# A graph attention kernel whose copies of the probabilities and first loads go out on two DMA queues, with sums and scalings moved ahead and another order at the end

## The chip, the cores and the metric

One Trainium2 chip, one of its cores. The metric is the time of one execution in microseconds (us); lower is better. A core has TensorE (PE in the profile), VectorE (DVE), ScalarE (ACT), GpSimd (POOL) and SyncE (SP), which run side by side and wait for each other on semaphores. SyncE computes nothing: it issues DMAs.

## The reference

128 graphs of 64 nodes, 512 features, 16 heads of 32. `adj` says which nodes see each other. Everything is float32, and all four biases are used.

```python
q = heads(x @ Wq + bq); k = heads(x @ Wk + bk); v = heads(x @ Wv + bv)
scores = jnp.einsum('bhqd,bhkd->bhqk', q, k) / sqrt(32)
scores = jnp.where(mask[:, None] == 0, -jnp.inf, scores)
attn = jax.nn.softmax(scores, axis=-1)
out = jnp.einsum('bhqk,bhkd->bhqd', attn, v)          # then the heads side by side
x = _layernorm(x + out @ Wo + bo)                     # no scale, no shift
```

## The kernel before

The 8192 rows are cut into 64 **tiles** of 128 rows (two graphs each). Four tiles make a group, for which q and k are projected together. Float32 products are made of three matmuls on a high and a low part (`split_matmul`, L252 to L254). The program is written out per engine; the order of each engine's instructions is the order of the code, and semaphores tie them together. There is no scheduler.

A tile c goes through these steps:

- PE `project_v`, `project_k`, `project_q` (L252 to L254); ACT `read_k` (L464) and `read_q` (L455) and DVE `read_v` (L546) take the results out of PSUM.
- PE `score` (L303); DVE `mask` (L554 adds the mask, L562 takes the row maximum); POOL `centre` (L706); ACT `exp` (L470); DVE `sum_up` (L566 sum, L569 reciprocal); POOL `normalise` (L163); DVE `turn` (L574, transposes 32x32 blocks).
- SP `place` (L189) issues eight DMAs of 64 KB that put the blocks of probabilities into the big zeroed buffer `pt`; PE `mix` (L317) multiplies it by v, and waits for all eight.
- ACT `read_ot` (L475, high part), DVE `split_ot` (L578, low part), PE `project_out` (L329, L330, L333).
- SP `load_row` (L195) fetches the rows of x, POOL `add_bo` (L701) adds the bias, DVE `add_row` (L585, L588, L591) adds the projection and takes mean and variance, POOL `make_rstd` (L711, L714), DVE `norm_row` (L595), SP `store` (L199).

The loop runs over 30 **slots** p, each with the tiles a = 2p and b = 2p + 1. In slot p PE scores a and b, mixes a-2 and b-2, and projects v for a and b, k and q for a+4 and b+4, and the output for a-2 and b-2. Tiles 60 to 63 have an end written out by hand. SP's queue holds, in this order, loads of adj and x (every second slot), store(a-3), place(a), load_row(b), place(b), store(a-2), load_row(b+1). The first loads (four pieces each of wq and x, then wk, biases, wv, adj, wo, x) are also SP's. `row` has four buffers: load_row(c) waits until tile c-4 is stored.

Of the kernel before, what the change touches and what calls it, by code (L numbers as in the profile page):

```python
# [39 lines left out]
def attention_kernel(nc, xt_dram, x_dram, adj_dram, w_dram, b_dram, out_dram):  # L40
    ctx = ExitStack()
    with ctx:
# [32 lines left out]
        stats = sb("stats", [P, 4, 6])  # L75
        moments = sb("moments", [P, 4, 2])
        shifted = sb("shifted", [P, 4, 1])
        rstd = sb("rstd", [P, 4, 1])
# [12 lines left out]
        row_in = [sem(f"row_in{n}") for n in range(4)]  # L91
        stored = [sem(f"stored{n}") for n in range(4)]
# [8 lines left out]
        turned = sem("turned")  # L101
# [33 lines left out]
        def ot_bank(c):  # L135
            if 2 * FULL <= c < 2 * FULL + 2:
                return psum_s[:, c % 2, 0, :]
            if c >= 2 * FULL + 2:
                return ring[c % 2][:, :]
            return at(c // 2 + 1, c % 2)  # L140
# [13 lines left out]

        def by_row_head(ap):
            return ap.rearrange("p b h k -> p h b k")
# [4 lines left out]
        def normalise(eng, ops, c):  # L161
            eng.wait_ge(inverted, c + 1)
            ops.tensor_tensor(soft_of(c), soft_of(c), on_keys(inverse[:, c % 2, :]), ALU.mult).then_inc(normed, 1)  # L163

        def by_graph(ap):
            return ap.rearrange("p (g k) -> p g k", k=NODES)

# [3 lines left out]
        def _(sp):  # L171
# [10 lines left out]
            def place(c):  # L182

                sp.wait_ge(turned, c + 1)
                wait_for(sp, mixed, c - 1)
                for q in range(P // SQ):
                    for k in range(2):
                        to = q // 2 * NODES + k * SQ
                        sp.dma_start(pt[to:to + SQ, c % 2, q, :, :],  # L189
                                     soft_of(c)[q * SQ:(q + 1) * SQ, k, :, :]).then_inc(pt_in[c % 2], DMA)  # L190

            def load_row(c):
                if c >= 4:
                    sp.wait_ge(stored[c % 4], DMA * (c // 4))
                sp.dma_start(row[:, c % 4], x_dram[c]).then_inc(row_in[c % 4], DMA)  # L195

            def store(c):
                sp.wait_ge(row_done, c + 1)
                sp.dma_start(out_dram[c], row[:, c % 4]).then_inc(stored[c % 4], DMA)  # L199

            for kc in range(KC):
                sp.dma_start(w_raw[0][:, kc, :], w_dram[0][:, kc, :]).then_inc(wq_in[kc], DMA)
                sp.dma_start(x_raw[:, kc, :], xt_dram[0, :, kc, :]).then_inc(x0_in[kc], DMA)
                if kc == 0:
                    for dst, src in zip((bq, bk), b_dram):
                        sp.dma_start(dst[:, :], src).then_inc(qk_b_in, DMA)
            for kc in range(KC):
                sp.dma_start(w_raw[1][:, kc, :], w_dram[1][:, kc, :]).then_inc(wk_in[kc], DMA)
            for dst, src in zip((bv, bo), b_dram[2:]):
                sp.dma_start(dst[:, :], src).then_inc(vo_b_in, DMA)  # L210
# [22 lines left out]
            T = TILES  # L233
            store(T - 7)
            place(T - 4)
            load_row(T - 3)
            place(T - 3)
            place(T - 2)
            place(T - 1)
            store(T - 6)  # L240
            load_row(T - 2)
            store(T - 5)
            load_row(T - 1)
            for c in range(T - 4, T):
                store(c)
# [4 lines left out]
        def _(pe):  # L250
# [179 lines left out]
            pe.wait_ge(row_added, T - 5)  # L430
            mix(T - 2)
            pe.wait_ge(row_added, T - 4)
# [7 lines left out]
        def _(act):  # L440
# [35 lines left out]

            def split_w(n, kc):
# [7 lines left out]

            for kc in range(KC):
# [28 lines left out]
            for p in range(FULL):  # L515
# [6 lines left out]
                for c in (a, b):  # L522
                    if c + 2 * GT < TILES:
                        split_x(c + 2 * GT)
                    read_k(c + GT)
                    read_q(c + GT)
# [3 lines left out]
            for c in range(T - 4, T):  # L530
                exp(c)
            for c in range(T - 4, T):
                read_ot(c)

        @block.vector
        def _(dve):
# [34 lines left out]
            def turn(c):  # L571
                dve.wait_ge(normed, c + 1)
# [9 lines left out]
            def add_row(c):  # L582
                dve.wait_ge(y_proj, c + 1)
                dve.wait_ge(row_biased, c + 1)
                nc.vector.tensor_tensor(row[:, c % 4, :], y_bank(c), row[:, c % 4, :],  # L585
                                        ALU.add).then_inc(row_added, 1)
                dve.wait_ge(row_added, c + 1)
                nc.vector.bn_stats(stats[:, c % 4, :], row[:, c % 4, :]).then_inc(row_stats, 1)  # L588
                dve.wait_ge(row_stats, c + 1)
                dve.sem_inc(dve_went_on, 1)  # L590
                nc.vector.bn_aggr(moments[:, c % 4, :], stats[:, c % 4, :]).then_inc(row_moments, 1)  # L591

            def norm_row(c):
                dve.wait_ge(row_rstd, c + 1)
                nc.vector.tensor_scalar(row[:, c % 4, :], row[:, c % 4, :], moments[:, c % 4, 0:1],  # L595
                                        rstd[:, c % 4, :], ALU.subtract, ALU.mult).then_inc(row_done, 1)
# [23 lines left out]
            for p in range(FULL):  # L620
# [20 lines left out]
                if p >= 1:  # L641
                    norm_row(a - 2)
# [7 lines left out]
            norm_row(T - 7)  # L650
            sum_up(T - 4)
            sum_up(T - 3)
# [9 lines left out]
            add_row(T - 5)  # L662
            turn(T - 1)
            norm_row(T - 6)
            norm_row(T - 5)
            read_v(T - 2)
            read_v(T - 1)
            split_ot(T - 4)
            split_ot(T - 3)
            add_row(T - 4)  # L670
            add_row(T - 3)
            split_ot(T - 2)
            norm_row(T - 4)
            split_ot(T - 1)
            norm_row(T - 3)
            add_row(T - 2)
            norm_row(T - 2)
            add_row(T - 1)
            norm_row(T - 1)

        @block.gpsimd
        def _(pool):
# [16 lines left out]
            def add_bo(c):  # L699
                pool.wait_ge(row_in[c % 4], DMA * (c // 4 + 1))  # L700
                nc.gpsimd.tensor_tensor(row[:, c % 4, :], row[:, c % 4, :], bo[:, :],  # L701
                                        ALU.add).then_inc(row_biased, 1)
# [6 lines left out]
            def make_rstd(c):  # L709
                pool.wait_ge(row_moments, c + 1)  # L710
                nc.gpsimd.tensor_tensor(shifted[:, c % 4, :], moments[:, c % 4, 1:2], eps[:, :],  # L711
                                        ALU.add).then_inc(row_shifted, 1)
                pool.wait_ge(row_shifted, c + 1)
                nc.gpsimd.tensor_tensor(rstd[:, c % 4, :], shifted[:, c % 4, :], minus_half[:, :],  # L714
# [18 lines left out]
            for p in range(FULL):  # L733
# [21 lines left out]
            add_bo(T - 4)  # L755
# [3 lines left out]
            centre(T - 1)  # L759
            add_bo(T - 3)  # L760
            normalise(pool, nc.gpsimd, T - 2)
            normalise(pool, nc.gpsimd, T - 1)
            make_rstd(T - 6)
            make_rstd(T - 5)
            add_bo(T - 2)
            add_bo(T - 1)
            for c in range(T - 4, T):
                make_rstd(c)

# [33 lines left out]
```

## Time and profile before

| | us |
|---|---|
| median of 3 runs | 880.45 |
| lowest, highest | 876.42, 881.17 |
| the profiled execution, time | 879.76 |
| its span, first to last instruction | 878.0 |

The profile is one execution. Its span leaves 1.8 us of its time outside. Busy times are of one engine; an engine that waits is not busy, and PE's matmuls overlap, so that a stretch in which PE shows no gap is one in which it is never waited for. The timeline's rows give the start and the length of a piece of work, and in brackets how long the engine had been idle before it and what ended that. A row of the SP queue (SPq) is the issuing of a DMA, not its transfer.

### The profile page before, as it was taken

How to read it: one execution, taken by the hardware profiler on the slowest of the kernel's cores; microseconds unless marked ns; L12 is line 12 of the kernel's file. 1: busy time of each engine (PE TensorE's matmuls, PEld its weight loads, DVE VectorE, ACT ScalarE, POOL GpSimd, SP SyncE). 2: the span in 40 equal slices, each digit the busy share in tenths (PEclk: the TensorE clock that was granted, in tenths of full speed). 3: DMA queues.
4: the chain of work that ended last, by engine and by line, in shares of the span. 5: the costliest groups of instructions: out<-in, count | busy, mean ns of one | idle time of the engine just before them, and what ended most of it. 6: DMA issues, size and time to landing. Idle time of an engine off the chain costs nothing.

```text
span 878.0 us, 17537 instructions
## 1 busy us (share of the span) xinstructions
PE 844.6 (96%) x7177; PEld 690.7 (79%) x7177; DVE 541.0 (62%) x729; ACT 285.5 (33%) x401; POOL 470.9 (54%) x409
## 2 busy tenths in 40 slices
PE   7979899999999999999999999999999999999973
PEld 6857788888888888888888888888888878888852
DVE  4655566655676655576655567665567665557863
ACT  6532333223333323333323333332333332323210
POOL 2254565546666455656545565654565654454632
PEclk9989999999999999999999999999999999999987
DMA  8224224343242433424243342434323243332143
GB/s 311 73 72 125 72 67 136 84 125 110 76 124 78 145 85 90 135 75 125 83 139 97 84 131 64 135 94 138 98 73 123 77 139 86 102 85 66 57 99 105
DMA packets 50143, 91.86 MB, mean 105 GB/s; under 512 B 11280, under 2 KB 13328, under 8 KB 47888
## 3 DMA queue, kind: packets, MB, share of 16 engines
q1 hardware_dynamic: 50064, 90.75, 35.1%
q8 instruction: 57, 0.93, 0.4%
q14 instruction: 22, 0.18, 0.1%
HBM read 40.37 MB, written 16.78 MB: 65 GB/s over the span
## 4 chain that ended last, share of the span: by engine, by line
PE 89%; DVE 3%; SPq 2%; DMA 2%; issue 2%; POOL 1%; ACT 1%; POOLq 0%; DVEq 0%; ACTq 0%
PE ring L252 20%; PE ring L253 19%; PE ring L254 19%; PE ring L317 6%; PE psum_s L303 6%; PE ring L329 6%; PE ring L333 6%; PE ring L330 6%; SPq L189 2%; DMA qt<-in_wq 1%; DMA row<-in_x 1%; DMA out_rows<-row 1%; DVE soft L554 1%; DVE top L562 0%; ACT kt L464 0%
## 5 line engine op out<-in xcount | busy, mean ns | idle before, releaser
L585 DVE TENSOR_TENSOR row<-ring,row 128x512 f32<-128x512 f32 x60 | 40.4, 673 | 207.5 <-PE ring L333 207.5
L701 POOL TENSOR_TENSOR row<-row,bo 128x512 f32<-128x512 f32 x64 | 88.4, 1381 | 138.9 <-DMA row<-in_x 138.9
L706 POOL TENSOR_TENSOR soft<-soft,top 128x1024 f32<-128x1024 f32 x62 | 118.9, 1917 | 80.5 <-DVE top L562 80.5
L163 POOL TENSOR_TENSOR soft<-soft,inverse 128x1024 f32<-128x1024 f32 x62 | 117.6, 1918 | 15.6 <-DVE inverse L569 15.6
L464 ACT ACTIVATE kt<-ring,bk_slot,in_slot 128x512 f32<-128x512 f32 x128 | 92.4, 773 | 81.9 <-PE ring L254 81.9
L252 PE MATMUL ring<-wv_hi,x_hi 128*128 128x512 f32 x256 | 104.0, 406 | 0.0
L252 PE MATMUL ring<-x_hi,wq_hi 128*128 128x512 f32 x256 | 99.8, 390 | 3.3 <-DVE x_lo L607 3.3
L574 DVE STREAM_TRANSPOSE soft<-soft 128x1024 f32<-128x1024 f32 x62 | 77.2, 1245 | 38.7 <-POOL soft L163 38.7
L253 PE MATMUL ring<-wv_lo,x_hi 128*128 128x512 f32 x256 | 101.0, 395 | 0.0
L254 PE MATMUL ring<-wv_hi,x_lo 128*128 128x512 f32 x256 | 100.9, 394 | 0.0
L252 PE MATMUL ring<-x_hi,wk_hi 128*128 128x512 f32 x256 | 99.8, 390 | 0.8 <-ACT kt L464 0.8
L253 PE MATMUL ring<-x_lo,wq_hi 128*128 128x512 f32 x256 | 99.6, 389 | 0.0
L253 PE MATMUL ring<-x_lo,wk_hi 128*128 128x512 f32 x256 | 99.6, 389 | 0.0
L254 PE MATMUL ring<-x_hi,wk_lo 128*128 128x512 f32 x256 | 99.6, 389 | 0.0
L254 PE MATMUL ring<-x_hi,wq_lo 128*128 128x512 f32 x256 | 99.5, 389 | 0.0
L470 ACT ACTIVATE soft<-soft 128x1024 f32<-128x1024 f32 x62 | 65.8, 1062 | 94.7 <-POOL soft L706 94.7
L329 PE MATMUL ring<-wo_hi,ot_hi 128*128 128x512 f32 x240 | 95.6, 398 | 0.0
L475 ACT CAST ot_hi<-ring 128x512 fp32r<-128x512 f32 x62 | 36.4, 587 | 178.6 <-PE ring L317 178.6
L330 PE MATMUL ring<-wo_lo,ot_hi 128*128 128x512 f32 x240 | 94.4, 393 | 0.0
L711 POOL TENSOR_TENSOR shifted<-moments,eps 128x1 f32<-128x1 f32 x64 | 12.2, 190 | 149.9 <-DVE moments L591 149.9
L554 DVE TENSOR_TENSOR soft<-psum_s,bias 128x1024 f32<-128x1024 f32 x62 | 75.6, 1220 | 7.6 <-DMA pt<-soft 7.2
L448 ACT CAST x_hi<-x_raw 128x512 fp32r<-128x512 f32 x60 | 36.6, 614 | 133.9 <-PE ring L254 131.1
(71 smaller groups left out, 1482.0 us busy)
## 6 DMA issues: line engine op xcount, KB each, us to landing
pt<-soft SPq DMA_DIRECT2D x496, 64.0 KB, 2.0
row<-in_x SPq DMA_DIRECT2D x64, 256.0 KB, 2.9
out_rows<-row SPq DMA_DIRECT2D x64, 256.0 KB, 2.3
x_raw<-in_xt SPq DMA_DIRECT2D x15, 1024.0 KB, 7.0
adj<-in_adj SPq DMA_DIRECT2D x16, 128.0 KB, 3.3
qt<-in_wq SPq DMA_DIRECT2D x4, 256.0 KB, 4.3
x_raw<-in_xt SPq DMA_DIRECT2D x4, 256.0 KB, 4.8
kt<-in_wk SPq DMA_DIRECT2D x4, 256.0 KB, 7.0
```

The lines of the kernel that those rows point to most:

```text
L163: ops.tensor_tensor(soft_of(c), soft_of(c), on_keys(inverse[:, c % 2, :]), ALU.mult).then_inc(normed, 1)
L252: nc.tensor.matmul(out, left_hi, right_hi, start=kc == 0, stop=False)
L253: nc.tensor.matmul(out, left_hi, right_lo, start=False, stop=False)
L254: return nc.tensor.matmul(out, left_lo, right_hi, start=False, stop=kc == KC - 1)
L329: nc.tensor.matmul(y_bank(c), ot_hi[:, c % 2, kc, :], w_hi[3][:, kc, :], start=kc == 0, stop=False)
L330: nc.tensor.matmul(y_bank(c), ot_hi[:, c % 2, kc, :], w_lo[3][:, kc, :], start=False, stop=False)
L464: last = nc.scalar.activation(kt[:, buf, m, :, s, :], by_graph(k_bank(J)), ACT.Identity, bias=bk_slot[:, s, m:m + 1], scale=in_slot[:, s:s ...
L470: nc.scalar.activation(soft_of(c), soft_of(c), ACT.Exp, scale=SCALE).then_inc(exped, 1)
L554: nc.vector.tensor_tensor(soft_of(c), psum_s[:, c % 2].rearrange("p r (h b k) -> p (r h) b k", b=2, k=SQ) .rearrange("p h b k -> p b h k") ...
L574: nc.vector.transpose(flat, flat).then_inc(turned, 1)
L701: nc.gpsimd.tensor_tensor(row[:, c % 4, :], row[:, c % 4, :], bo[:, :], ALU.add).then_inc(row_biased, 1)
L706: nc.gpsimd.tensor_tensor(soft_of(c), soft_of(c), on_keys(top[:, c % 2, :]), ALU.subtract).then_inc(centred, 1)
```

## The change

- The eight DMAs of `place` are shared: SP issues the four for q = 0 and 1, ACT the four for q = 2 and 3 (new function `place` on ACT, between the two halves of its slot's projection reads). `mix` waits for all eight as before.
- The first eight loads alternate between SP and ACT. The loads of bq and bk come after wk.
- In a slot, DVE's sum_up(a) comes before read_v(a), norm_row(a-3) after sum_up(b), and POOL's add_bo(a) after the two normalise.
- The end: the four last rows have buffers in `qt` (free once tile 59 is scored) and are loaded at once; stats and moments have eight buffers; DVE scales the probabilities of tile 63; turns come earlier and the additions of rows later; the norms of tiles 58 to 61 are POOL's; mix(62) and mix(63) write to other banks and no longer wait for `row_added`.

```diff
+        def row_of(c):
+            if c >= TILES - 4:
+                return qt[:, 0, c - (TILES - 4), :]
+            return row[:, c % 4, :]
...
+        def norm_row(eng, ops, c):
+            eng.wait_ge(row_rstd, c + 1)
+            ops.tensor_scalar(row_of(c), row_of(c), moments[:, c % 8, 0:1], rstd[:, c % 8, :],
+                              ALU.subtract, ALU.mult).then_inc(row_done, 1)
 # SP
-                for q in range(P // SQ):
+                for q in range(2):
...
             for kc in range(KC):
-                sp.dma_start(w_raw[0][:, kc, :], w_dram[0][:, kc, :]).then_inc(wq_in[kc], DMA)
-                sp.dma_start(x_raw[:, kc, :], xt_dram[0, :, kc, :]).then_inc(x0_in[kc], DMA)
-                if kc == 0:
-                    for dst, src in zip((bq, bk), b_dram):
-                        sp.dma_start(dst[:, :], src).then_inc(qk_b_in, DMA)
+                if kc % 2 == 0:
+                    sp.dma_start(w_raw[0][:, kc, :], w_dram[0][:, kc, :]).then_inc(wq_in[kc], DMA)
+                else:
+                    sp.dma_start(x_raw[:, kc, :], xt_dram[0, :, kc, :]).then_inc(x0_in[kc], DMA)
 ...
             def load_row(c):
+                if c >= TILES - 4:
+                    sp.wait_ge(scored, TILES - 4)
+                    sp.dma_start(row_of(c), x_dram[c]).then_inc(last_row_in[c % 4], DMA)
+                    return
...
             T = TILES
+            load_row(T - 3)
+            load_row(T - 2)
+            load_row(T - 1)
             store(T - 7)
-            place(T - 4)
-            load_row(T - 3)
-            place(T - 3)
-            place(T - 2)
-            place(T - 1)
-            store(T - 6)
-            load_row(T - 2)
-            store(T - 5)
-            load_row(T - 1)
             for c in range(T - 4, T):
+                place(c)
+            for c in range(T - 6, T):
                 store(c)
# PE, the end
-            pe.wait_ge(row_added, T - 5)
             mix(T - 2)
-            pe.wait_ge(row_added, T - 4)
             mix(T - 1)
# ACT
+            def place(c):
+                act.wait_ge(turned, c + 1)
+                wait_for(act, mixed, c - 1)
+                for q in range(2, 4):
+                    for k in range(2):
+                        to, of = block_of(c, q, k)
+                        act.dma_start(to, of).then_inc(pt_in[c % 2], DMA)
 ...
+            for kc in range(KC):
+                if kc % 2 == 0:
+                    act.dma_start(x_raw[:, kc, :], xt_dram[0, :, kc, :]).then_inc(x0_in[kc], DMA)
+                else:
+                    act.dma_start(w_raw[0][:, kc, :], w_dram[0][:, kc, :]).then_inc(wq_in[kc], DMA)
# DVE, a slot
+                sum_up(a)
+                if p >= 1:
                     read_v(a)
+                sum_up(b)
                 if p >= 2:
-                    norm_row(a - 3)
-                sum_up(a)
-                sum_up(b)
+                    norm_row(dve, nc.vector, a - 3)
# DVE, the end
             mask(T - 2)
+            turn(T - 4)
             mask(T - 1)
-            turn(T - 4)
+            turn(T - 3)
             read_v(T - 3)
-            turn(T - 3)
             sum_up(T - 2)
             sum_up(T - 1)
-            add_row(T - 6)
+            normalise(dve, nc.vector, T - 1)
             turn(T - 2)
# POOL, a slot
-                add_bo(a)
                 normalise(pool, nc.gpsimd, a)
                 normalise(pool, nc.gpsimd, b)
+                add_bo(a)
 # POOL, the end
-            for c in range(T - 4, T):
+            for c in range(T - 6, T - 2):
                 make_rstd(c)
+                norm_row(pool, nc.gpsimd, c)
+            make_rstd(T - 2)
+            make_rstd(T - 1)
```

The order of the instructions at the three places that matter most. First ACT in slot 0, before: `x_hi` is split_x(8) and (9), `kt` read_k, `qt` read_q of tiles 4 and 5.

```order
L448 CAST x_hi<-x_raw 128x4x128 [waits q_proj,v_proj,x_in]
L464 ACTIVATE kt<-ring,bk_slot,in_slot 128x8x64 [waits k_proj]
L464 ACTIVATE kt<-ring,bk_slot,in_slot 128x8x64
L455 ACTIVATE qt<-ring,bq 128x512 [waits q_proj]
L448 CAST x_hi<-x_raw 128x4x128 [waits q_proj,v_proj]
L464 ACTIVATE kt<-ring,bk_slot,in_slot 128x8x64 [waits k_proj]
L464 ACTIVATE kt<-ring,bk_slot,in_slot 128x8x64
L455 ACTIVATE qt<-ring,bq 128x512 [waits q_proj]
```

No DMA stands between them.

ACT in slot 0 with the change: the four rows of DMA for tile 0 and for tile 1 stand ahead of the second half.

```order
L465 CAST x_hi<-x_raw 128x4x128 [waits q_proj,v_proj,x_in]
L481 ACTIVATE kt<-ring,bk_slot,in_slot 128x8x64 [waits k_proj]
L481 ACTIVATE kt<-ring,bk_slot,in_slot 128x8x64
L472 ACTIVATE qt<-ring,bq 128x512 [waits q_proj]
L501 DMA pt<-soft 32x512 [waits turned]
L501 DMA pt<-soft 32x512 x3
L501 DMA pt<-soft 32x512 [waits turned]
L501 DMA pt<-soft 32x512 x3
L465 CAST x_hi<-x_raw 128x4x128 [waits q_proj,v_proj]
L481 ACTIVATE kt<-ring,bk_slot,in_slot 128x8x64 [waits k_proj]
L481 ACTIVATE kt<-ring,bk_slot,in_slot 128x8x64
L472 ACTIVATE qt<-ring,bq 128x512 [waits q_proj]
```

Split_x(9), read_k(5) and read_q(5) now come behind two waits for `turned`.

ACT at the end, before: read_ot(58) and (59), exp of tiles 60 and 61 (`soft`), of 62 and 63 (`x_raw`), then the four read_ot.

```order
L475 CAST ot_hi<-ring 128x512 [waits y_proj,mixed] x2
L470 ACTIVATE soft<-soft 128x1024 [waits centred] x2
L470 ACTIVATE x_raw<-x_raw 128x1024 [waits centred] x2
L475 CAST ot_hi<-psum_s 128x512 [waits y_proj,mixed] x2
L475 CAST ot_hi<-ring 128x512 [waits y_proj,mixed] x2
```

The first row is read_ot(58) and (59); all DMAs of the place are SP's here.

ACT at the end with the change, from the exp of tiles 60 and 61.

```order
L487 ACTIVATE soft<-soft 128x1024 [waits centred] x2
L501 DMA pt<-soft 32x512 [waits mixed,turned]
L501 DMA pt<-soft 32x512 x3
L487 ACTIVATE x_raw<-x_raw 128x1024 [waits centred]
L501 DMA pt<-soft 32x512 [waits mixed,turned]
L501 DMA pt<-soft 32x512 x3
L487 ACTIVATE x_raw<-x_raw 128x1024 [waits centred]
L492 CAST ot_hi<-psum_s 128x512 [waits y_proj,mixed]
L501 DMA pt<-x_raw 32x512 [waits mixed,turned]
L501 DMA pt<-x_raw 32x512 x3
L492 CAST ot_hi<-psum_s 128x512 [waits y_proj,mixed]
L501 DMA pt<-x_raw 32x512 [waits mixed,turned]
```

Each `place` stands between an exp or a read_ot and the next; exp(62) is now behind the wait for tile 60's turn.

DVE near the end, before: the norms of tiles 58 and 59 (first row), read_v(62) and (63), the low parts and the rows of tiles 60 and 61.

```order
L595 TENSOR_SCALAR row<-row,moments,rstd 128x512 [waits row_rstd] x2
L546 TENSOR_TENSOR v<-ring,bv 128x512 [waits mixed,v_proj] x2
L578 TENSOR_TENSOR ot_lo<-psum_s,ot_hi 128x512 [waits ot_hi_done] x2
L585 TENSOR_TENSOR row<-psum_s,row 128x512 [waits row_biased,y_proj]
L588 BN_STATS stats<-row 128x6 [waits row_added]
L591 BN_AGGR moments<-stats 128x2 [waits row_stats]
L585 TENSOR_TENSOR row<-psum_s,row 128x512 [waits row_biased,y_proj]
L588 BN_STATS stats<-row 128x6 [waits row_added]
L591 BN_AGGR moments<-stats 128x2 [waits row_stats]
L578 TENSOR_TENSOR ot_lo<-ring,ot_hi 128x512 [waits ot_hi_done]
L595 TENSOR_SCALAR row<-row,moments,rstd 128x512 [waits row_rstd]
L578 TENSOR_TENSOR ot_lo<-ring,ot_hi 128x512 [waits ot_hi_done]
```

The last two rows are the norm of tile 60 and the low part of tile 63.

DVE there with the change: it starts with the scaling of tile 63.

```order
L176 TENSOR_TENSOR x_raw<-x_raw,inverse 128x1024 [waits inverted]
L621 STREAM_TRANSPOSE x_raw<-x_raw 128x1024 [waits normed]
L625 TENSOR_TENSOR ot_lo<-psum_s,ot_hi 128x512 [waits ot_hi_done]
L621 STREAM_TRANSPOSE x_raw<-x_raw 128x1024 [waits last_normed]
L625 TENSOR_TENSOR ot_lo<-psum_s,ot_hi 128x512 [waits ot_hi_done]
L590 TENSOR_TENSOR v<-ring,bv 128x512 [waits mixed,v_proj] x2
L632 TENSOR_TENSOR row<-ring,row 128x512 [waits row_biased,y_proj]
L634 BN_STATS stats<-row 128x6 [waits row_added]
L637 BN_AGGR moments<-stats 128x2 [waits row_stats]
L632 TENSOR_TENSOR row<-ring,row 128x512 [waits row_biased,y_proj]
L634 BN_STATS stats<-row 128x6 [waits row_added]
L637 BN_AGGR moments<-stats 128x2 [waits row_stats]
```

No row of norms is left here; the turns of tiles 62 and 63 stand ahead of read_v and of all rows, and the rows of 58 and 59 behind them.

## Rows read from the trace of the kernel before

**Rows 1.** Stretches; length, busy time of each engine, granted clock, DMA share, GB/s

```profile
9.00:10.00 1.00, 0.88 (x4) 0.78 (x5) 1.00 (x2) 0.59 (x1) 0.00 (x0) 1.00 0.89 229
...
56.00:58.00 2.00, 0.00 (x0) 0.00 (x0) 0.00 (x0) 0.00 (x0) 2.00 (x2) 0.50 0.43 98
...
400.00:600.00 200.00, 200.00 (x1754) 164.83 (x1747) 130.47 (x176) 66.65 (x93) 116.64 (x98) 1.00 0.35 103
```

**Rows 2.** Timeline of the SP queue, start; start us, us, engine line op

```profile
4.95 0.43 SPq L203 DMA_DIRECT2D x_raw<-in_xt  x1
...
46.25 5.03 SPq L189 DMA_DIRECT2D pt<-soft  x8
```

**Rows 3.** Timeline of ACT, start; in brackets the idle time before

```profile
10.94 0.62 ACT L484 CAST wq_hi<-qt 128x512 fp32r<-128x512 f32 x1 [1.35 <-DMA qt<-in_wq]
```

**Rows 4.** Timeline of PE, start to tile 2

```profile
13.05 0.47 PE L252 MATMUL ring<-x_hi,wq_hi 128*128 128x512 f32 x1 [0.94 <-DVE x_lo L607]
...
14.28 0.39 PE L254 MATMUL ring<-x_hi,wq_lo 128*128 128x512 f32 x1
...
58.39 1.93 PE L317 MATMUL ring<-pt,v 128*32 128x128 f32 x32 [4.54 <-issue]
60.25 0.80 PE L252 MATMUL ring<-wv_hi,x_hi 128*128 128x512 f32 x1
...
62.51 0.40 PE L254 MATMUL ring<-wv_hi,x_lo 128*128 128x512 f32 x1
```

**Rows 5.** Timeline of PE, 86 to 92 us

```profile
89.99 0.65 PE L317 MATMUL ring<-pt,v 128*32 128x128 f32 x5 [2.72 <-issue]
```

**Rows 6.** Timelines of DVE, SP, ACT and PE, one slot in the middle

```profile
413.77 1.25 DVE L574 STREAM_TRANSPOSE soft<-soft 128x1024 f32<-128x1024 f32 x1 [0.63 <-POOL soft L163]
418.84 4.94 SPq L189 DMA_DIRECT2D pt<-soft  x8
420.05 1.45 ACT L464 ACTIVATE kt<-ring,bk_slot,in_slot 128x512 f32<-128x512 f32 x2 [2.10 <-PE ring L254]
427.36 1.96 PE L317 MATMUL ring<-pt,v 128*32 128x128 f32 x64
```

**Rows 7.** Timeline of PE, the end

```profile
839.84 1.08 PE L317 MATMUL psum_s<-pt,v 128*32 128x128 f32 x32 [1.38 <-issue]
845.56 1.93 PE L317 MATMUL psum_s<-pt,v 128*32 128x128 f32 x32 [4.64 <-issue]
...
868.77 2.08 PE L333 MATMUL psum_s<-wo_hi,ot_lo 128*128 128x512 f32 x4 [4.31 <-DVE ot_lo L578]
```

**Rows 8.** Timeline of the SP queue, the end

```profile
845.85 11.13 SPq L189 DMA_DIRECT2D pt<-x_raw  x16
```

**Rows 9.** Timeline of POOL, the end

```profile
842.64 3.78 POOL L163 TENSOR_TENSOR x_raw<-x_raw,inverse 128x1024 f32<-128x1024 f32 x2
...
865.50 1.26 POOL L701 TENSOR_TENSOR row<-row,bo 128x512 f32<-128x512 f32 x1 [2.00 <-DMA row<-in_x]
```

**Rows 10.** The page, part 5: the exponential, all of it

```profile
L470 ACT ACTIVATE soft<-soft 128x1024 f32<-128x1024 f32 x62 | 65.8, 1062 | 94.7 <-POOL soft L706 94.7
```

**Rows 11.** One line of the kernel, the mask of a group: durations

```profile
L696 POOL TENSOR_SCALAR bias<-adj x16: 1077/1084/1093, 18.8 to 778.1; 128x256 f32<-128x256 int32 x16
```

**Rows 12.** Timeline of DVE, the end

```profile
836.41 1.16 DVE L566 TENSOR_REDUCE total<-x_raw 128x16 f32<-128x1024 f32 x1
...
844.58 1.25 DVE L574 STREAM_TRANSPOSE x_raw<-x_raw 128x1024 f32<-128x1024 f32 x1 [5.12 <-POOL x_raw L163]
...
867.57 0.55 DVE L595 TENSOR_SCALAR row<-row,moments,rstd 128x512 f32<-128x512 f32 x1 [9.86 <-POOL rstd L714]
...
869.09 0.69 DVE L585 TENSOR_TENSOR row<-psum_s,row 128x512 f32<-128x512 f32 x1
...
870.65 0.18 DVE L591 BATCH_NORM_AGGREGATE moments<-stats 128x2 f32<-128x6 f32 x1
...
874.89 0.55 DVE L595 TENSOR_SCALAR row<-row,moments,rstd 128x512 f32<-128x512 f32 x1 [0.93 <-POOL rstd L714]
```

More of the change, by code:

```diff
@@ L74, in attention_kernel @@
         inverse = sb("inverse", [P, 2, HEADS])
[L75 to L78, printed above, removed]
+        stats = sb("stats", [P, 8, 6])
+        moments = sb("moments", [P, 8, 2])
+        shifted = sb("shifted", [P, 8, 1])
+        rstd = sb("rstd", [P, 8, 1])
         eps = sb("eps", [P, 1])
@@ L91, in attention_kernel @@
         row_in = [sem(f"row_in{n}") for n in range(4)]
+        last_row_in = [sem(f"last_row_in{n}") for n in range(4)]
         stored = [sem(f"stored{n}") for n in range(4)]
@@ L521, in _ @@
                 exp(b)
[L522 to L526, printed above, removed]
+                if a + 2 * GT < TILES:
+                    split_x(a + 2 * GT)
+                read_k(a + GT)
+                read_q(a + GT)
+                place(a)
+                place(b)
+                if b + 2 * GT < TILES:
+                    split_x(b + 2 * GT)
+                read_k(b + GT)
+                read_q(b + GT)
             T = TILES
@@ L529, in _ @@
             read_ot(T - 5)
-            for c in range(T - 4, T):
-                exp(c)
-            for c in range(T - 4, T):
-                read_ot(c)
+            exp(T - 4)
+            exp(T - 3)
+            place(T - 4)
+            exp(T - 2)
+            place(T - 3)
+            exp(T - 1)
+            read_ot(T - 4)
+            place(T - 2)
+            read_ot(T - 3)
+            place(T - 1)
+            read_ot(T - 2)
+            read_ot(T - 1)
         @block.vector
@@ L584, in add_row @@
                 dve.wait_ge(row_biased, c + 1)
-                nc.vector.tensor_tensor(row[:, c % 4, :], y_bank(c), row[:, c % 4, :],
-                                        ALU.add).then_inc(row_added, 1)
+                nc.vector.tensor_tensor(row_of(c), y_bank(c), row_of(c), ALU.add).then_inc(row_added, 1)
                 dve.wait_ge(row_added, c + 1)
-                nc.vector.bn_stats(stats[:, c % 4, :], row[:, c % 4, :]).then_inc(row_stats, 1)
+                nc.vector.bn_stats(stats[:, c % 8, :], row_of(c)).then_inc(row_stats, 1)
                 dve.wait_ge(row_stats, c + 1)
                 dve.sem_inc(dve_went_on, 1)
[L591 to L596, printed above, removed]
+                nc.vector.bn_aggr(moments[:, c % 8, :], stats[:, c % 8, :]).then_inc(row_moments, 1)
             def split_w(n, kc):
@@ L641, in _ @@
                 if p >= 1:
-                    norm_row(a - 2)
+                    norm_row(dve, nc.vector, a - 2)
             T = TILES
@@ L699, in add_bo @@
             def add_bo(c):
[L700 to L702 removed]
+                if c >= TILES - 4:
+                    pool.wait_ge(last_row_in[c % 4], DMA)
+                else:
+                    pool.wait_ge(row_in[c % 4], DMA * (c // 4 + 1))
+                nc.gpsimd.tensor_tensor(row_of(c), row_of(c), bo[:, :], ALU.add).then_inc(row_biased, 1)
             def centre(c):
@@ L754, in _ @@
             centre(T - 3)
-            add_bo(T - 4)
             normalise(pool, nc.gpsimd, T - 4)
@@ L759, in _ @@
             centre(T - 1)
+            add_bo(T - 4)
+            normalise(pool, nc.gpsimd, T - 2)
             add_bo(T - 3)
[L761 to L764, printed above, removed]
             add_bo(T - 2)
             add_bo(T - 1)
-            for c in range(T - 4, T):
+            for c in range(T - 6, T - 2):
                 make_rstd(c)
+                norm_row(pool, nc.gpsimd, c)
+            make_rstd(T - 2)
+            make_rstd(T - 1)
 def kernel(x, adj, L0_gnn_Wq, L0_gnn_bq, L0_gnn_Wk, L0_gnn_bk, L0_gnn_Wv, L0_gnn_bv, L0_gnn_Wo, L0_gnn_bo):
```

51 lines of the change are left out of this document (28 added, 23 removed).

## The prediction

> **What bounds the kernel now.** I read the busy time by stretches first. In the middle PE is the bound: from 400 to 600 us it is busy for 200.00 of 200 us at full clock [rows 1], and DVE, ACT and POOL have room. The reader should see that no saving on them can shorten that stretch. PE waits for more than 1.5 us in three places only, found in its timeline. At the start the four pieces of wq and x come in one by one; the last piece of wq lets ACT go on at 10.94 us, and PE's first matmul on it starts at 13.05 [rows 3, 4]. In slot 1 mix(1) starts after 4.54 us of idle PE, in slot 2 some matmuls of a mix after 2.72 [rows 4, 5]. And in the end mix(61) comes after 4.64 us, and the last part of project_out(62) after 4.31 [rows 7].
>
> The waits of slot 1 and of the end have one cause. A tile's eight copies go out one after another on SP, 0.6 us each: those of tile 0 take 5.03 us from 46.25, then a row load and the eight of tile 1 follow, and 2.1 us after the start of the last one (56.3) mix(1) starts at 58.39 [rows 2, 4]. The last 16 copies of the kernel take 11.13 us of SP's time [rows 8]. The last wait is another: the loads of rows 62 and 63 queue on SP behind stores, POOL adds the bias at 865.50, and DVE sits 9.86 us before norm_row(60), with the low part of tile 62 behind it, which PE waits for [rows 7, 9, 12].
>
> **The change, part by part.** The sum is made against the profiled execution, 879.76 us for a span of 878.0; the median of the runs, 880.45, is 0.7 above it. Times below are on the clock of the trace before. I take the four issues of each queue at the 0.63 us of SP, side by side: 2.5 us a tile.
>
> *First loads.* The last of the eight is issued at 4.95 [rows 2]; with four on each queue that would be about 2.4 us sooner, the upper end. But from 9 to 10 us the DMA engines are busy for 0.89 of the time and move 229 GB/s [rows 1]: the pieces wait for transfers, not for issues. Lower end 0. I take 1.0, nearer to the busy engines. The table load of ACT now follows its four issues and is done when the first piece arrives; bq and bk come later, with about 5 us to spare before PE asks for q(0) out of PSUM. Nothing for either. The Trainium skill (DMA: Bandwidth & Descriptors, section on issuing engines) speaks against a gain here: all queues run on the same 16 DMA engines, and a second one saves issue time only. By that rule this term is 0.
>
> *Slot 0 and 1.* Normalise(0) no longer waits for add_bo(0), so turn(0) and the first copies move from 46.25 to 45.8. SP then issues four copies, the row, four copies: to 51.4, the last begun at 50.8 and landed 2.1 later, at 52.9. ACT issues its eight from 45.8 to 50.8, and only then splits x(9) (0.62) and reads k(5) (1.45, as in rows 6): 52.9. Mix(1) needs both, and PE reaches it at 53.4, after the scores and mix(0). So it starts 5.0 us sooner. There is more: in the idle time the granted clock fell to 0.50, that is from 2.4 to 1.2 GHz, after PE had been idle for some 3 us [rows 1], mix(1) took 1.93 for what takes 1.08 at the end of the trace [rows 4, 7], and the five matmuls from 60.25 took 2.26 us where those from 13.05 took 1.23 [rows 4]. Without the gap that is 1.9 us. **Slot 1: 6.9 us**, 5.0 if the clock still falls.
>
> *Slot 2.* The 2.72 us have the releaser "issue", in the midst of a mix, while x of a later group is loading: no data was missing. PE's own instructions do not change there. The loads of x now go out some 4 us sooner against PE, so the pause may stay or go. With the slow matmuls behind it, it is worth 0 to 3.9; I take the middle, 1.9, since no row is near either end.
>
> *The middle slots.* Nothing gained: PE has no wait. Is the cover kept? In the slot shown turn(b) ends at 415.0 and ACT's next work that waits for PE, read_k(b+4), starts at 420.05 after 2.10 us of idle [rows 6]. With sums and scalings moved ahead turn(a) ends about 412.6, so ACT's eight issues (5.0) run to 417.7 or so, split_x(b+8) follows, and ACT is free 1.7 us before read_k is due. SP has fewer issues than before. POOL's add_bo(a) moves behind 3.8 us of scaling [rows 9], and its sum is asked for in the next slot. Cost 0.
>
> *The end.* PE works without a wait until 838.5 (839.84 less 1.38) [rows 7]. Then:
>
> 1. Turn(60) moves ahead of mask(63), to 831.0; both queues issue to 833.6; landed by 835.7. Mix(60) starts at 838.5.
> 2. Turn(61) ends at 834.5, its copies have landed at 839.2. Mix(61) starts at 839.5, not at 845.56.
> 3. ACT does exp(63) behind these copies, to 838.3 (1.06) [rows 10]; DVE adds up (1.4 with the reciprocal) and scales tile 63 itself (1.2, as its turn of the same size) instead of waiting for two scalings of POOL, 3.78 [rows 9, 12]; the turns of 62 and 63 end at 842.3 and 844.2, not at 845.8 and 848.6.
> 4. ACT: copies of 62, read_ot(61) to 845.4, copies of 63 to 847.9; landed at 849.9, where the last landed at about 858.5 before.
> 5. PE: project_out(60) to 844.0, (61) to 848.2, mix(62), mix(63) to 850.9, project_out(62) to 853.8, (63) to 856.8.
> 6. DVE, from 846.1: two read_v 1.3, five add_row of 1.7 (869.09 to 870.83) [rows 12], two split_ot 0.7 each. The moments of tile 58 are there at 849.1, those of 62 at 857.3.
> 7. POOL then does rstd (0.9 with its wait, the idle time before the last norm) and norm_row for four tiles in a row. The trace has no such norm on POOL. The nearest rows are its addition of the same width, 1.26, and its tensor_scalar of half that width, 1.08 [rows 9, 11]; twice the latter, 2.2, is the upper end, 1.08 the lower. I take 1.3, the same width. Norm(61) ends at 857.7, rstd(62) at 858.5; DVE then has norm 0.5, add_row(63) 1.7 and a wait of 0.9, and the last norm starts at 861.7, not at 874.89.
>
> The store behind the last norm is as before. **The end: 13.2 us**; 9.6 with a norm of 2.2, 13.6 with 1.08 (DVE is then the bound).
>
> **Sum:** 1.0 + 6.9 + 1.9 + 13.2 = 23.0, so 879.8 - 23.0 = 856.8, **857 us**. With all lower ends (0, 5.0, 0, 9.6) it is 865.2, with all upper ends (2.4, 6.9, 3.9, 13.6) 853.0.
>
> **The rivals.**
>
> - *Nothing at the start.* The loads are bound by transfers alone: 857.8. For it the 0.89 [rows 1]; against it, 229 GB/s is little for engines so busy, and two queues may mix better. Chance 0.20. By the Trainium skill's page on DMA, section on issuing engines, it would be this one.
> - *Dear norms on POOL.* At 2.2 us each they hold the end: 860.4. Chance 0.12.
> - *More pauses like that of slot 2.* PE now runs from tile 0 without the idle time of slot 1, in which its instructions could catch up. Three more at 3.9 give about 869. Against it: one such pause over 1 us in 30 slots. Chance 0.06.
> - *Issuing is shared.* If the two queues slow each other, and an issue costs twice 0.63, ACT is done with the copies of tile 1 at 55.9 and with k(5) at 57.9 (gain 0.5), the last copies are issued at 857.6, and the last norm starts about 867.8 (gain 7.1): 872. No row shows two queues at once. Chance 0.14.
> - *The copies do not land sooner.* If landing, not issuing, sets the pace of 0.6 us a copy, the change does not do what it says: 877 to 880. Against it, 64 KB each 0.63 us is 104 GB/s, and the same engines moved 229. Chance 0.04.
> - *Slower: ACT's queue blocks the middle.* Behind the two waits for `turned` and the eight issues stand split_x(b+8) and read_k(b+4), and the next slot's second mix, at 428.3 (halfway through the pair at 427.36) [rows 6], waits for that k. The issues start at 412.6, 2.1 us of work follow, so they may take 13.6 us: 1.7 each. Beyond that each slot stalls. At 2.0 us each it is 2.4 us in each of 29 slots, +70, less what the end keeps: about 920. For it: no row shows ACT issuing. Against it: SP's issues stay near 0.6, 4.94 for eight [rows 6]. Chance 0.04.
>
> **How the numbers follow.** The forecast has 0.40, the others as given; the sum is 1. A measurement of this kernel tells 0.5%, 4.4 us, from no change. Faster by more than that: 0.92; within: 0.04; slower: 0.04. The range goes from 852, one below the upper ends, to 870, which takes in the dear norms, the pauses and the near part of the shared issuing.
>
> **What would show it.** Mix(1) within 1 us of mix(0), no clock of 0.50 before 800 us unless at slot 2, ACT's DMA issues 0.5 to 0.7 us, read_k(b+4) in the middle still waiting for PE, PE's gaps behind 838 adding up to under 4 us in place of 13, and a chain at the end that runs through POOL's norms. Wrong if ACT's issues last over 1 us, if PE shows gaps in the middle slots, or if the piece of wq that comes last still comes at 10.9 and slot 1 still waits.

## The result, and the profile after

The changed kernel takes **859.12 us** (median of four executions, 857.66 to 859.69) where the kernel before takes 880.21 (four, 876.42 to 881.17): a ratio of 0.9769, 95% interval 0.9740 to 0.9799. It is faster by 21 us, and 2.1 us above the 857.0 that was predicted. Measured again later it took 859.66 (six executions) beside 875.74 of the kernel before (eleven, 874.14 to 882.07): 0.9794, interval 0.9757 to 0.9830. The kernel before has executions near 875 (six of these eleven) and others near 880, its profiled one, 879.76, among them, so that the gain is 16 us by the later measurement and 21 by the first.

The profiled execution of the change took 857.66 us with a span of 855.9, 22.1 less than the 878.0 before. I split both spans where PE starts the scores of a pair of tiles, which it does once in each slot:

| stretch (us) | before | after | gain | predicted |
|---|---|---|---|---|
| start to the first score | 33.64 | 32.38 | 1.26 | 1.0 |
| slot 0 | 16.85 | 16.83 | 0.02 | 0 |
| slot 1 | 32.94 | 25.96 | 6.98 | 6.9 |
| slot 2 | 30.51 | 25.96 | 4.55 | 1.9 |
| the other slots (25.96 each, but one of 26.88 and 26.30) | | | 0.58 | 0 |
| the end, from the last full pair's score (815.78, 802.39) | 62.19 | 53.47 | 8.7 | 13.2 |

So the sum came out by luck, by two errors that cancel: slot 2 gave 2.65 more than its term, the end 4.5 less.

**Start.** The windows of the changed kernel, one in the first loads and one in the middle (columns as in [rows 1]):

```profile
9.00:10.00 1.00, 1.00 (x6) 0.81 (x5) 0.62 (x2) 0.31 (x1) 0.00 (x0) 1.00 1.06 402
...
386.60:586.60 200.00, 200.00 (x1760) 165.08 (x1760) 130.02 (x175) 66.03 (x92) 116.59 (x98) 1.00 0.34 101
```

Between 9 and 10 us the DMA engines now move 402 GB/s, not 229. In the middle nothing moved: PE is busy for all of the 200 us. ACT's timeline at the start answers to [rows 3]:

```profile
2.12 0.64 ACTq L516 DMA_DIRECT2D qt<-in_wq  x1
2.79 1.28 ACT L510 ACT_TABLE_LOAD   x1 [2.79 <-issue]
4.74 0.62 ACT L510 CAST wq_hi<-qt 128x512 fp32r<-128x512 f32 x1 [0.67 <-DMA qt<-in_wq]
...
9.69 0.62 ACT L510 CAST wq_hi<-qt 128x512 fp32r<-128x512 f32 x1 [0.88 <-DMA qt<-in_wq]
...
14.51 1.26 ACT L472 ACTIVATE qt<-ring,bq 128x512 f32<-128x512 f32 x2 [1.47 <-POOL bk_slot L769]
```

The first piece is split later than before (4.74 for 3.87), the last one 1.25 us sooner. The last row shows a new wait: bk is issued later, and ACT waits 1.47 us for what POOL makes of it. PE does not.

**Slot 0 to 1.** Both queues and PE, which answer to [rows 2, 4]:

```profile
44.31 2.49 SPq L207 DMA_DIRECT2D pt<-soft  x4
...
47.47 2.51 SPq L207 DMA_DIRECT2D pt<-soft  x4
```

```profile
44.31 5.39 ACTq L501 DMA_DIRECT2D pt<-soft  x8
49.80 0.62 ACT L465 CAST x_hi<-x_raw 128x512 fp32r<-128x512 f32 x1 [5.73 <-PE ring L273]
50.33 1.44 ACT L481 ACTIVATE kt<-ring,bk_slot,in_slot 128x512 f32<-128x512 f32 x2
```

```profile
49.80 1.38 PE L322 MATMUL psum_s<-kt,qt 64*64 64x128 f32 x44
51.11 1.95 PE L336 MATMUL ring<-pt,v 128*32 128x128 f32 x64
```

Two queues issue side by side at 0.63 and 0.67 us each, and mix(0) and mix(1) run as one group of 64 matmuls, with no idle time and at full clock.

**The end.** The chain of waits of the changed kernel from 821 us (start, us, what), a part of it:

```profile
821.09 0.52 ACTq L501
821.63 0.87 ACTq L501
822.53 0.62 ACTq L501
823.18 0.62 ACTq L501
823.84 1.07 ACT x_raw L487
824.94 1.23 DVE total L610
826.19 0.26 DVE inverse L613
826.48 2.13 DVE x_raw L176
828.61 1.17 DVE x_raw L621
...
832.62 0.59 ACT ot_hi L492
...
837.79 2.08 POOL row L183
...
840.78 2.08 POOL row L183
...
843.76 2.08 POOL qt L183
...
846.73 2.08 POOL qt L183
```

exp(63) stands behind four copies on ACT, DVE's scaling of tile 63 takes 2.13 us (1.92 on POOL), and four norm_rows of 2.08 us follow each other on POOL. On DVE the last norm comes out of that chain, after 5.07 us of idle time:

```profile
849.64 0.55 DVE L183 TENSOR_SCALAR qt<-qt,moments,rstd 128x512 f32<-128x512 f32 x1 [5.07 <-POOL rstd L755]
...
852.77 0.55 DVE L183 TENSOR_SCALAR qt<-qt,moments,rstd 128x512 f32<-128x512 f32 x1 [0.93 <-POOL rstd L755]
```

PE in the end, answering to [rows 7]:

```profile
825.00 1.95 PE L336 MATMUL psum_s<-pt,v 128*32 128x128 f32 x64
...
830.39 1.19 PE L352 MATMUL psum_s<-wo_hi,ot_lo 128*128 128x512 f32 x4 [1.38 <-DVE ot_lo L625]
...
833.26 0.50 PE L348 MATMUL psum_s<-wo_hi,ot_hi 128*128 128x512 f32 x1 [1.67 <-ACT ot_hi L492]
...
838.34 1.08 PE L336 MATMUL ring<-pt,v 128*32 128x128 f32 x32 [1.01 <-DMA pt<-x_raw]
```

The waits for mixes 60 and 61 are gone. Three are left, 4.06 us in all, two of them new: split_ot(60) stands behind turn(62) on DVE, and read_ot(61) behind the copies of tile 62 on ACT.

### The profile page after: what moved, and what is told of

It is laid out like the page before. It is cut to its first block, busy times and chain, and to the rows that moved or that the text cites. A ratio compares the mean times of both kernels' runs of the same rounds, so it can differ in the third digit from the quotient of the medians.

```text
span 855.9 us, 17597 instructions
## 1 busy us (share of the span) xinstructions
PE 837.0 (98%) x7177; PEld 686.9 (80%) x7177; DVE 540.7 (63%) x726; ACT 284.5 (33%) x401; POOL 480.3 (56%) x412
## 4 chain that ended last, share of the span: by engine, by line
PE 91%; DVE 4%; POOL 2%; issue 1%; DMA 1%; ACTq 1%; ACT 1%; POOLq 0%; DVEq 0%
PE ring L271 20%; PE ring L272 19%; PE ring L273 19%; PE psum_s L322 6%; PE ring L336 6%; PE ring L348 6%; PE ring L352 6%; PE ring L349 6%; DMA qt<-in_wq 1%; ACTq L501 1%; DVE soft L598 1%; POOL qt L183 0%; POOL row L183 0%; DVE top L606 0%; DVE total L610 0%
## 5 line engine op out<-in xcount | busy, mean ns | idle before, releaser
L176 POOL TENSOR_TENSOR soft<-soft,inverse 128x1024 f32<-128x1024 f32 x62 | 123.3, 1989 | 25.1 <-DVE inverse L613 22.1
L743 POOL TENSOR_TENSOR row<-row,bo 128x512 f32<-128x512 f32 x60 | 78.8, 1313 | 38.5 <-DMA row<-in_x 38.5
```

What stands on the lines that cost most here:

```text
L743: nc.gpsimd.tensor_tensor(row_of(c), row_of(c), bo[:, :], ALU.add).then_inc(row_biased, 1)
```

## The experiments

**x1: first loads on two queues, alone** (in the kernel before).

```diff
+                if kc % 2 == 0:
+                    act.dma_start(x_raw[:, kc, :], xt_dram[0, :, kc, :]).then_inc(x0_in[kc], DMA)
+                else:
+                    act.dma_start(w_raw[0][:, kc, :], w_dram[0][:, kc, :]).then_inc(wq_in[kc], DMA)
```

(SP keeps the other four, and bq and bk move behind wk, as in the change.)

> The kernel before with the first eight loads on two queues and bq, bk after wk, nothing else. Theory (issuing sooner brings the pieces sooner): the first score starts at 32.4 us in place of 33.64, as in the changed kernel, and the rest is as before: slot 1 still 32.9 us from score to score, the end still 62 us behind the last slot's score; span about 876.7. Rival (transfers alone bind, and the 1.3 us in the changed kernel came from something else): first score at 33.6, span 878. The pause of slot 2 (4.55 us) should be there in both, if it comes with the idle time of slot 1; if it depends on chance it may be gone.

One execution: 880.66 us, span 878.9, no sooner than the kernel before. The first score is at 33.22 (33.64 before), not at the 32.4 that I had put, and ACT's timeline has the gain at its last piece:

```profile
9.76 0.62 ACT L485 CAST wq_hi<-qt 128x512 fp32r<-128x512 f32 x1 [0.70 <-DMA qt<-in_wq]
```

What it gained is lost in slot 2, where the pause is still there and the clock stays low behind it:

```profile
89.57 0.65 PE L318 MATMUL ring<-pt,v 128*32 128x128 f32 x5 [2.98 <-issue]
90.15 0.80 PE L253 MATMUL ring<-wv_hi,x_hi 128*128 128x512 f32 x1
```

One trace is too little for 1 us. Over all profiles of this study the last piece of wq is split at 10.52 to 11.05 us in the four kernels with one queue, at 9.36 to 9.76 in the six with two, and the first score is at 33.29 to 33.79 (mean 33.57) and at 32.08 to 33.22 (mean 32.67). The ranges do not overlap, though those of the first score are only 0.07 us apart: the difference of the means, 0.9 us, is what the term is worth here.

**x2: copies on two queues, alone** (in the kernel before; ACT's order as in the change, first loads, DVE, POOL and row buffers as before).

```diff
-                for q in range(P // SQ):
+                for q in range(2):
...
+            def place(c):
...
+                for q in range(2, 4):
```

> The kernel before with the eight copies of a tile shared by SP and ACT and ACT's order as in the changed kernel; loads, DVE, POOL and PE as before. Theory (serial issuing on one queue made the wait of slot 1): slot 1 takes 26.0 us from score to score in place of 32.94, mix(1) right behind mix(0), no clock of 0.50 there; in the end the last block is issued 5.6 us sooner, and with it the loads of rows 62 and 63, so the end is about 5 us shorter. Together 12 us, and 16.5 if the pause of slot 2 goes too: 864 to 868. Rival (the sums and scalings moved ahead made the gain): slot 1 keeps a gap of over 3 us, time over 873.

862.64 us (862.31 to 865.32; four executions, beside 877.24 of the kernel before in seven), ratio 0.9830, interval 0.9790 to 0.9869. The span is 860.1, so the copies alone bring 17.9 of the 22.1 us between the profiled executions: slot 1 lasts 26.78, slot 2 26.83, the end 54.76 (7.4 less than before). That is below my 864 to 868, mostly because the end gives 7.4 and not 5. Of the 17.9 us 3.7 are the pause of slot 2, which is not the same in every execution (see x6). PE's timeline has what is left in slots 1 and 2:

```profile
54.01 1.08 PE L317 MATMUL ring<-pt,v 128*32 128x128 f32 x32 [0.61 <-DMA pt<-soft]
...
81.48 0.42 PE L317 MATMUL ring<-pt,v 128*32 128x128 f32 x5 [0.46 <-issue]
```

**x3: the change with all copies on SP.**

```diff
-                for q in range(2):
+                for q in range(4):
...
-                place(a)
-                place(b)
```

(ACT's place goes altogether.)

> The changed kernel with all eight copies of a tile on SP, ACT issuing none of them; everything else as changed. Theory: slot 1 is long again (32.3 to 32.9 us from score to score, mix(1) some 4 us behind mix(0), clock 0.50), 6.5 us lost there; the middle stays at 25.96 us a slot; the end loses 3 us on mix(61) and mix(63), but its last norm hangs on the four norms on POOL, so it loses 0 to 3 us. If the pause of slot 2 comes with the idle time of slot 1, 4.5 more. Time 866 to 873. Rival (the sharing does nothing, the earlier sums do all): 859.

865.50 us (864.37 to 870.63; four executions), ratio 0.9864, interval 0.9822 to 0.9907; span 862.6. Slot 1 is at 31.92 again. The time is just under my 866 to 873, since the end got shorter. The idle time before mix(1) is back, and with it the low clock:

```profile
56.13 1.94 PE L336 MATMUL ring<-pt,v 128*32 128x128 f32 x32 [4.19 <-issue]
...
836.98 1.24 PE L336 MATMUL psum_s<-pt,v 128*32 128x128 f32 x32 [2.98 <-issue]
```

The surprise is the end. PE waits 2.98 us before mix(61), and yet the end lasts 52.26 us, 1.2 less than with two queues. exp(63) starts 19.51 us after the last full pair's score, against 21.45 in the change, since no copies stand ahead of it on ACT, and DVE's scaling of tile 63 takes 1.55 us, not 2.13: the turns of 62 and 63 end 2.5 us sooner. The second queue helps PE in the end, but PE does not set the end.

**x5: the idle time of slot 1 filled** (the kernel before with 18 matmuls whose results nobody reads, ahead of mix(1); one execution, 874.50 us, span 872.7). Does the low clock cost 1.9 us there?

```diff
+                if p == 1:
+                    for _ in range(18):
+                        nc.tensor.matmul(ring[1][:, :], w_hi[3][:, 0, 0:P], w_hi[3][:, 0, :], start=True, stop=True)
                 mix(b - 2)
```

> The kernel before with 18 matmuls of 128x512 (results unused) on PE between mix(0) and mix(1) in slot 1, about 4.1 us of work inside the wait. Theory of the clock: mix(1) still starts at about 58.4, as its copies come no sooner, but runs at full clock: its 32 matmul records take 1.08 us in place of 1.93, and five matmuls behind it 1.2 in place of 2.26; slot 1 is 1.9 us shorter, 31.0. For the pause of slot 2: if it comes from PE having been idle in slot 1, it is gone and slot 2 takes 25.96 us (span about 871.6); if it comes from the load of x that falls on it, it stays (span about 876).

Slot 1 lasts 32.04, not 31.0. PE's timeline:

```profile
53.93 4.38 PE L387 MATMUL ring<-wo_hi 128*128 128x512 f32 x18
59.47 1.08 PE L317 MATMUL ring<-pt,v 128*32 128x128 f32 x32 [1.16 <-DMA pt<-soft]
60.48 0.50 PE L252 MATMUL ring<-wv_hi,x_hi 128*128 128x512 f32 x1
```

Mix(1) takes 1.08 us where it took 1.93, and five matmuls from 60.48 take 1.26 where [rows 4] have 2.26: together the 1.9 us of the prediction. The size of the clock's cost is shown. But the copies of tile 1 landed 1.1 us later in this execution (SP's eight took 5.83 us, not 4.94), so mix(1) began later and half of it was lost. A second thing was not expected: slot 2 lasts 25.96. Its pause is gone.

**x6: the pause of slot 2.** In the traces of before, x1, x2 and x3 the pause sits at the same matmul of PE, 3.84 us behind the first score of the slot; in x5 it is missing. The queue that brings instructions, q8 (57 packets, 0.93 MB in all, 16 KB each), goes with it: in the four with a pause a packet starts 2.5 to 3.8 us after the first packet of the 1 MB load of x (87.51 against 85.01 in the kernel before), and PE goes on 1.2 to 1.6 us behind the packet's end; in x5 it came at 73.88, long before the load (85.36), in the changed kernel at 73.48, as the load began (73.43). The DMA views of the kernel before, from 80 to 87.3 and from 87.3 to 89 us (issues; packets, MB and share by queue). In the first there is a load of x and no row of q8:

```profile
x_raw<-in_xt SPq DMA_DIRECT2D x1, 1024.0 KB, 7.1
```

In the second there is one packet of it:

```profile
q1 hardware_dynamic: 51, 0.32, 51.7%
q8 instruction: 1, 0.02, 3.3%
```

To test it the load of x for group 3 brings 16 columns; x of tiles 12 to 15 is left out otherwise.

```diff
+                if G == 3:
+                    sp.dma_start(x_raw[:, 0, 0:16], xt_dram[G, :, 0, 0:16]).then_inc(x_in, DMA)
+                    return
```

> The kernel before, in which the 1 MB load of x for group 3 (issued in slot 2) brings 16 of its columns only; it leaves out x of tiles 12 to 15 otherwise. Theory (PE waits for its next block of instructions, which comes behind that load on the same DMA engines): the pause of 2.98 us at 88.9 goes or falls under 0.6, slot 2 lasts 26 to 27.5 us in place of 30.5, slot 1 stays at 32.9. Rival (the pause follows from the idle time and the low clock of slot 1, whatever is loading): slot 2 stays at 30 to 31. The time falls by 3 to 4.5 us by the first, by nothing by the second.

Slot 2 lasts 26.25 us while slot 1 is at 33.51: all but 0.3 us of the pause is gone though the idle time ahead of it is not, and the rival falls. The packet came at 85.10, 1.5 us into the slot, where it came 4.1 us into it in the kernel before. PE's timeline has both mixes of slot 2 as one group, which takes 2.24 us in place of 1.95:

```profile
83.63 1.98 PE L306 MATMUL psum_s<-kt,qt 64*64 64x128 f32 x64
85.54 2.24 PE L320 MATMUL ring<-pt,v 128*32 128x128 f32 x64
```

That a late packet makes the pause is borne out by the other traces: it is short where the packet comes 1.4 to 2.0 us into the slot (x2, x4, x6, x7, a2: slot 2 at 26.24 to 26.83), and long where it comes 2.3 to 4.5 us into it (x3, before, x1: 27.62 to 32.2). That the load makes the packet late is not shown. In x4, x7 and a2 the load stands ahead of the packet, and the packet comes within 0.1 us of where it does in x6. In slot 26 of the kernel before (26.88 us) PE pauses 0.52 us at the same place, and the packet there starts 1.1 us ahead of the load. And a2 is the changed kernel itself, of which the first trace has no pause in slot 2:

```profile
80.12 0.42 PE L336 MATMUL ring<-pt,v 128*32 128x128 f32 x5 [0.28 <-issue]
```

So when the packet comes differs between executions of one kernel, and a single one of x6 can't tell the missing load from that. Its time, 875.22 us, is 4.5 below the profiled execution of before, but equal to those of its eleven that lie near 875. The pause may well be what parts the two sorts of executions; only one execution of the kernel before has a profile, so this is argued and not shown.

**x4: the end's norms on DVE.** The change, but norm_row of tiles 58 to 61 goes from POOL to DVE, each two or three steps behind its add_row; POOL keeps make_rstd.

```diff
-            for c in range(T - 6, T - 2):
+            for c in range(T - 6, T):
                 make_rstd(c)
-                norm_row(pool, nc.gpsimd, c)
-            make_rstd(T - 2)
-            make_rstd(T - 1)
```

> After the change, with all norm_rows of the end on DVE (0.5 us each there) between its additions, and POOL left with make_rstd alone. Theory (the four norms of 2.08 us on POOL, one behind the other, hold the end): the last norm_row starts 3.3 to 3.9 us sooner than 852.77, so the span is about 852.3 and the time about 855.7. Rival (DVE with its additions of 1.7 us is the bound, so what leaves POOL only comes back on DVE): 857.5 or more, no change. PE's part of the end stays as it is, its last matmul at about 845.2.

855.20 us, with 854.72, 855.20 and 855.88 in three executions (a fourth took 1694.79 and is left out), ratio 0.9743, interval 0.9696 to 0.9790; span 852.9. The end lasts 49.82 us, 3.65 less than the change's 53.47, as the theory had it; the rival falls. DVE's timeline:

```profile
842.33 0.53 DVE L183 TENSOR_SCALAR row<-row,moments,rstd 128x512 f32<-128x512 f32 x1
...
849.83 0.55 DVE L183 TENSOR_SCALAR qt<-qt,moments,rstd 128x512 f32<-128x512 f32 x1 [0.71 <-POOL rstd L759]
```

The same operation takes 0.53 us there and 2.08 on POOL. PE's part stays as it was: its last matmul ends 43.1 us after the last full pair's score, in the change 42.8.

**x7: another order of the end, on top of x4.** It is aimed at exp(63), PE's waits and the scaling. The edit against the change, in part:

```diff
-            place(T - 3)
             exp(T - 1)
+            place(T - 3)
             read_ot(T - 4)
-            place(T - 2)
             read_ot(T - 3)
+            place(T - 2)
...
             sum_up(T - 2)
+            turn(T - 2)
             sum_up(T - 1)
-            normalise(dve, nc.vector, T - 1)
-            turn(T - 2)
             split_ot(T - 4)
-            turn(T - 1)
             split_ot(T - 3)
             read_v(T - 2)
             read_v(T - 1)
+            turn(T - 1)
```

(And the scaling of tile 63 back on POOL, all norms on DVE as in x4, in a slightly other order among the additions.)

> After the change, with another order in the end: exp(63) before the copies of tile 61 and read_ot(61) before those of tile 62 on ACT, the scaling of tile 63 on POOL again and DVE's turn(62) before sum_up(63), and all norms on DVE as in the run before. Theory (the end is 3.5 us too long by POOL's norms, and PE waits 1.38, 1.67 and 1.01 us because split_ot(60) stands behind turn(62) and read_ot(61) behind four issues): PE's waits behind mix(61) fall from 4.1 us to 2 or less, the span is about 849 and the time about 852. Rival (PE's waits only move to mix(62) and mix(63), since the turns of 62 and 63 come later): 855 to 856, as with the norms alone.

**853.42 us** (852.22 to 855.36, six executions), ratio 0.9725, interval 0.9691 to 0.9759. It is faster than both kernels: the change beside it took 858.91 to 861.15, and the two sets do not meet (0.993 of its median). The end lasts 46.72 us, another 3.1 less. The waits of PE behind mix(61) fall from 4.06 us to one of 2.40, somewhat more than I had put:

```profile
834.02 1.08 PE L336 MATMUL ring<-pt,v 128*32 128x128 f32 x32
837.51 1.08 PE L336 MATMUL ring<-pt,v 128*32 128x128 f32 x32 [2.40 <-DMA pt<-x_raw]
```

It is mix(63) that waits, 2.40 us where it waited 1.01 in the change: so the rival was right in part. Turn(63) now stands behind both read_v and ends at 832.48, and the copies of tile 63 follow it:

```profile
831.25 1.23 DVE L621 STREAM_TRANSPOSE x_raw<-x_raw 128x1024 f32<-128x1024 f32 x1
```

```profile
828.41 7.56 ACTq L501 DMA_DIRECT2D pt<-x_raw  x8
```

The ACT row spans its eight issues for tiles 62 and 63, with 1.5 us of waiting for that turn between them. The four for tile 63 take 3.45 us, where eight take 5.39 in slot 0.

**a2: the change once more**, for that comparison.

> The changed kernel once more, beside these on the same chip: 857.7 to 859.7 us.

859.66 us (858.91 to 861.15), span 857.9: first score 33.16, slot 2 26.65, end 53.45. The end is the same to 0.02 us in two profiles; the 2 us between the spans are at the start, in slot 2 and in one later slot.

## Why the prediction was right, and where it was not

*First loads, 1.0: right.* 1.26 in the profile, 0.9 over all of them. The rival "nothing at the start" falls. The Trainium skill (DMA: Bandwidth & Descriptors, section "Issuing engines are not separate DMA queues") says that a second engine saves only the time to issue, usually a small one. The traces do not contradict that: the last of the eight issues starts at 2.12 in place of 4.95, and the last piece of wq is split 0.8 to 1.7 us sooner. What they do not bear out is the 0 that the prediction made of it. Whether issues set the gain or the order in which the pieces share the engines was not tried.

*Slot 1, 6.9: right, and for the reason given.* 6.98. x3 has the wait of 4.19 us back with one queue, and x5 shows the clock's part. What x2 leaves of it, 0.61 us before mix(1), is gone in the change, where the sums and scalings come sooner. One reading was off: the granted clock was 0.81 from 55 to 56 us and 0.50 from 56 on, so that it fell some 1.8 us after PE's last work (53.85), not some 3; in x3 it held to about 56.1, 4 us after. ACT was free of its eight copies at 49.7 and of k(5) at 51.8. The rival "issuing is shared" falls, since an issue costs 0.67 us on ACT beside SP, not 1.3, and so does "the copies do not land sooner".

*Slot 2, 1.9: undersized.* 4.55 in the profile against a term of 0 to 3.9. The step that failed is "PE's own instructions do not change there", with the middle taken for want of a row. The instructions do not change, but when a packet of them arrives does, and it sets the pause (the traces under x6). The upper bound was too low as well: without the pause slot 2 is at 25.96, and 30.51 less that was there to be read. Part of the gain is luck: a2, the same kernel, has slot 2 at 26.65, a gain of 3.9. Why the packet comes early in one execution and late in another, and what the load has to do with it, is open. By the Trainium skill (Runtime: NRT & Kernel Launch, section "Instruction fetch mechanics") instructions come in 16 KiB blocks fetched ahead, a cost "mostly hidden"; the middle slots, at 25.96, agree, and the 2.72 and 2.98 us of before and x1 do not. "More pauses" did not come: no later slot is longer than 26.30 us.

*Middle, 0: right.* The slots are at 25.96. ACT's eight issues run from 399.55 to 405.4 in one of them, and read_k then waits 1.14 us for PE: the cover held, with half of the margin it had. The rival of the other sign falls by the 0.73 us of an issue there, against the 1.7 from which it decides. (Its price, "about 920", does not follow from its terms: 879.8 and 70, less all of the 23.0, are 927.)

*The end, 13.2: oversized by 4.5.* Two terms were mis-sized. Norm_row on POOL was taken at 1.3 us, "the same width" as the addition; it is 2.08, near the upper end of 2.2. Four in a row are 3.1 us of the 4.5. x4 takes them away and gains 3.65. The rival "dear norms" is what happened, at its place and price; it was given 0.12 on 860.4. DVE's scaling of tile 63 was taken at 1.2 us "as its turn of the same size"; it is 2.13, more than POOL's 1.92, and the turns come 0.9 and 0.7 later. With them the copies of tile 62 on ACT and read_ot(61) behind them come later (done at 833.2, where my schedule less the 13.4 us by which the two scores differ has 832.0), then split_ot(61), and the moments of tile 58 1.1 us later than worked out. 1.1 and 3.4 (the norms with what lies between them) are the 4.5. The 3.1 us that the end loses once more in x7 came from several moves at once; which of them gave how much was not tried.

*The sum:* 23.0 worked out, 22.1 measured; the errors are +0.3 (start), +0.1, +2.6, +0.6 and -4.5.

*The parts overlap.* Between single profiled executions the copies alone (x2) give 17.9 us, the rest without them (x3) 15.4, and together 22.1; 3.7, 2.9 and 4.6 of these are the pause of slot 2. In the end each gives 7.4 and 9.9, together 8.7: once the copies are quick other things bound the end, and ACT's exp(63) comes 1.9 us later for the copies ahead of it.

## What to carry to other kernels

Before an operation moves to another engine, look for a row of just that operation on that engine: width alone is no guide (the norm: 0.53 us on DVE, 2.08 on POOL; the scaling: 1.92 on POOL, 1.55 to 2.14 on DVE). Where an engine takes over DMA issues, ask what stands behind them in its queue at the end of the program, where nothing else covers them. A pause with no missing data is to be looked for in the instruction queue. And one trace of each kernel is too little for a gain of a few us where such a pause comes and goes.

## What was not expected of the hardware

- A tensor_scalar with two per-partition operands, 128x512, takes 2.08 us on POOL, an addition of two full tensors of that size 1.3.
- A multiplication by a broadcast operand, 128x1024, takes 2.13 us on DVE in the change (2.14 in x4 and a2) and 1.55 in x3, which is unexplained; on POOL it takes 1.92 at the median of 62:

```profile
L176 POOL TENSOR_TENSOR soft<-soft,inverse x62: 1915/1921/2072, 40.9 to 814.4; 128x1024 f32<-128x1024 f32 x62
...
L176 DVE TENSOR_TENSOR x_raw<-x_raw,inverse x1: 2130/2130/2130, 826.5 to 826.5; 128x1024 f32<-128x1024 f32 x1
```

- PE stood for 0.2 to 3.0 us, always at the same matmul of slot 2, where a 16 KB packet of instructions started 1.4 to 4.5 us into the slot, and went on 1.2 to 1.6 us behind the packet's end.
- Issues of 64 KB copies take 0.59 us on SP and 0.61 on ACT at the median of the middle, side by side, and single ones up to 1.85 and 1.58 us (the change, 192 on each queue from 150 to 780 us).
